# The opening of a gated cross-attention and expert layer: tiles 0 and 1 multiplied before they are scaled, and a new split of the contexts' low parts

## The reference

```python
x = x + tanh(g_xattn) * xattn(layernorm(x), itok, ctx, ctx, ctx)
x = x + tanh(g_ffn) * ffn(layernorm(x), ...)
# xattn: each token has one of 4 experts e, by its id
g = silu(h @ ctx[e].T)
u = h @ ctx[e].T
y = (g * u) @ ctx[e].T
```

## Time and profile before

| | us |
|---|---|
| median of 3 runs | 477.32 (476.93 to 477.61) |
| the profiled execution, its time | 476.73 |
| its span, first to last instruction | 474.9 |
| busy: TensorE (PE), its weight loads (PEld) | 458.2, 393.2 |
| busy: VectorE (DVE), ScalarE (ACT), GpSimd (POOL) | 316.9, 268.1, 212.5 |
| mean granted clock of TensorE | 0.996 |

### The profile page before, as it was taken

How to read it: one execution, slowest core, us unless ns; L and a number is a source line. 1 busy time by engine, 2 the same in 40 slices (tenths; PEclk the granted TensorE clock), 3 DMA queues, 4 the chain that set the end, 5 groups by cost and what they waited for, 6 DMA issues and landing times.

```text
span 474.9 us, 7916 instructions
## 1 busy us (share of the span) xinstructions
PE 458.2 (96%) x2493; PEld 393.2 (83%) x2493; DVE 316.9 (67%) x789; ACT 268.1 (56%) x417; POOL 212.5 (45%) x175
## 2 busy tenths in 40 slices
PE   2999999999999999999999999999999999999993
PEld 1478888888888888888889999999999999999982
DVE  6679888878876554479469776566666676666520
ACT  4766556666564643633345676566655577656431
POOL 0513444664543475426168354443435455443242
PEclk9999999999999999999999999999999999999998
DMA  8643874776664542254289999889879998888555
GB/s 297 196 171 126 267 262 165 235 257 205 241 209 151 179 155 95 55 68 63 35 230 172 284 307 270 252 272 287 268 197 262 247 274 273 266 245 223 110 63 72
DMA packets 29166, 95.04 MB, mean 200 GB/s; under 512 B 4816, under 2 KB 5328, under 8 KB 28624
## 3 DMA queue, kind: packets, MB, share of 16 engines
q0 software_dynamic: 17040, 43.66, 37.4%
q1 hardware_dynamic: 11808, 50.98, 32.1%
q10 hardware_dynamic: 288, 0.01, 0.0%
HBM read 67.50 MB, written 28.70 MB: 203 GB/s over the span
## 4 chain that ended last, share of the span: by engine, by line
PE 95%; ACT 1%; DVE 1%; DMA 1%; POOLq 0%; POOL 0%; issue 0%
PE psG L1314 51%; PE psY L1314 32%; PE psT L1319 8%; PE psG L1572 1%; PE psG L1343 1%; DMA tok_i<-in_ids 1%; PE psY L1331 1%; ACT arena L563 0%; POOLq L81 0%; ACT arena L554 0%; PE psY L1450 0%; PE psG L1344 0%; POOL out L513 0%; PE psY L1476 0%; PE psG L1319 0%
## 5 line engine op out<-in xcount | busy, mean ns | idle before, releaser
L1314 PE MATMUL psY<-arena 128*128 (+1 forms) x372 | 90.8, 394 | 0.0
L1314 PEld LDWEIGHTS psY<-arena 128*128 128x128 f32 x372 | 68.7, 188 | 14.1 <-issue 0.2
L504 POOL DMA_INDIRECT ht<-out,idx x32 | 33.7, 1052 | 59.0 <-PE psT L1319 43.2
L1314 PE MATMUL psY<-slot,arena 128*128 128x512 f32 x240 | 58.8, 394 | 0.0
L1089 DVE TENSOR_TENSOR slot<-raw,slot 128x1536 fp32r<-128x1536 f32 x25 | 43.9, 1757 | 19.5 <-ACT slot L635 19.5
L1314 PE MATMUL psG<-arena 128*128 x228 | 56.8, 398 | 0.0
L1089 DVE TENSOR_TENSOR arena<-raw,arena 128x1536 fp32r<-128x1536 f32 x24 | 42.0, 1758 | 16.4 <-ACT arena L635 16.3
L1314 PEld LDWEIGHTS psY<-slot,arena 128*128 128x128 f32 x240 | 44.2, 188 | 9.2 <-ACT xh_sb L679 0.3
L1314 PE MATMUL psG<-arena,slot 128*128 128x512 f32 x216 | 51.3, 392 | 0.0
L1314 PEld LDWEIGHTS psG<-arena 128*128 128x128 f32 x228 | 41.5, 188 | 8.3 <-issue 0.4
L750 ACT ACTIVATE s_sb<-psG 128x224 f32<-128x224 f32 (+1 forms) x48 | 17.6, 366 | 54.6 <-PE psG L1314 54.6
(11 more groups left out here) (231 smaller groups left out, 814.6 us busy)
## 6 DMA issues: line engine op xcount, KB each, us to landing
raw<-in_w SPq DMA_DIRECT2D x51, 768.0 KB, 5.9
padded<-xh_sb SPq DMA_DIRECT2D x19, 256.0 KB, 2.3
raw<-in_ctx_t SPq DMA_DIRECT2D x2, 1024.0 KB, 8.7
ht<-in_ctx_t SPq DMA_DIRECT2D x1, 1024.0 KB, 11.7
xh_sb<-in_ctx_t SPq DMA_DIRECT2D x1, 1024.0 KB, 7.1
out<-log_sb SPq DMA_DIRECT2D x4, 256.0 KB, 7.6
ht<-out,idx POOLq DMA_INDIRECT x32, 5.2
xb<-in_x,idx POOLq DMA_INDIRECT x19, 3.8
```

The costliest lines, as they stand in the source:

```text
L504: pool.indirect_dma_start(ht[:, n, :], None, halves_of_out, slots(e * NA + a, 0)).then_inc(g_here[n], 16)
L1314: ins = pe.matmul(ps, left[a], right[b], start=n == 0 and m == 0, stop=n == total - 1 and m == 2)
```

## The change

- Tiles 0 and 1 are no longer normalised ahead of their product. VectorE subtracts the mean only (`centre`) into h; ScalarE's and VectorE's passes behind the product take the root as a scale (`silu1`, `gate1`, with `r01`). Their normalising on ScalarE goes. The roots of tiles 0 and 1 are taken as a pair, those of tile 2 alone.
- Tile 1 has its own buffers for its transposed parts (`hT1` in bl0) and bank for its product (psG[1]); TensorE's transposition of tile 1 stands in the middle of tile 0's product, tile 1's product directly behind.
- Low parts: contexts 0 and 1 half by VectorE (`low_ctx(0, 1, 2)`, `low_ctx(1, 0, 2)`, first in its queue) and half by TensorE, two pieces each; context 2 in two halves by VectorE; context 3 whole by VectorE in step 2, ahead of tile 4's statistics, with gate 2 and the low part of tile 3 ahead of it. Four of TensorE's eight pieces go.
- ScalarE takes context 2's high part in two halves, and context 3's directly behind tile 0's SiLU; then come tile 0's gT, tile 2's normalising, and so on.
- Context 3 is loaded into raw, over context 0, and waits for that context's low part besides.
- The steps begin at t = 1; what is before them is written out.

```diff
-            for t in range(FIRST, LAST):
+            for t in range(1, LAST):
...
+        hT1 = [bl0[:, n * KD * P:(n + 1) * KD * P] for n in range(2)]
+        def hT_of(t):
+            return hT1 if t == 1 else hT
+        def p_bank(t):
+            return psG[1 if t == 1 else 0][:, :]
...
         def ctx_raw(e):
-            if e < 2:
-                return raw_flat[:, e * KD * D:(e + 1) * KD * D]
-            return (ht if e == 2 else xh_sb)[:, :, :].rearrange("p a d -> p (a d)")
+            if e == 2:
+                return ht[:, :, :].rearrange("p a d -> p (a d)")
+            return raw_flat[:, e % 3 * KD * D:(e % 3 + 1) * KD * D]
...
-            for e in range(E1 - 1):
+            for e in range(E1):
+                if e == E1 - 1:
+                    sp.wait_ge(xa_here[2], 16)
+                    sp.wait_ge(ctx_lo_done, 1)
                 sp.dma_start(ctx_raw(e), ctx_t[e, :, :]).then_inc(ctx_here[e], 16)
-            sp.wait_ge(xa_here[2], 16)
-            sp.dma_start(ctx_raw(E1 - 1), ctx_t[E1 - 1, :, :]).then_inc(ctx_here[E1 - 1], 16)
...
-            def take_rest(e, i):
-                act.wait_ge(rest_ps, e // 2 * KD + i + 1)
-                if e and i == KD - 1:
-                    act.wait_ge(ctx_lo_done, 2)
-                o = (e * KD + i) * D
+            def take_rest(i):
+                act.wait_ge(rest_ps, i + 1)
+                if i % 2:
+                    act.wait_ge(ctx_half, i // 2 + 1)
+                o = (i // 2 * KD + i) * D
                 act.activation(ctx_lo[:, o:o + D], psG[i][:, :],
-                               ACT.Copy).then_inc(rest_taken if i < KD - 1 else ctx_lo_done, 1)
-            high_ctx(0)
-            high_ctx(1)
-            take_rest(0, 0)
-            take_rest(0, 1)
-            high_ctx(2)
-            take_rest(0, 2)
-            take_rest(0, 3)
+                               ACT.Copy).then_inc(ctx_lo_done if i % 2 else rest_taken, 1)
+            def half_ctx(e, n):
+                act.wait_ge(ctx_here[e], 16)
+                c = slice(n * KD * D // 2, (n + 1) * KD * D // 2)
+                ins = act.activation(ctx_hi[:, e * KD * D:(e + 1) * KD * D][:, c], ctx_raw(e)[:, c], ACT.Copy)
+                if n:
+                    ins.then_inc(ctx_hi_done, 1)
...
+            def hT_high(t):
+                act.wait_ge(hT_ps, t + 1)
+                act.activation(hT_of(t)[0], psT[0][:, :], ACT.Copy).then_inc(hT_hi, 1)
+            def silu1(t):
+                act.wait_ge(p_ps, t + 1)
+                if t:
+                    act.wait_ge(gu_ready, t)
+                if t < 2:
+                    act.wait_ge(r01_ready, t + 1)
+                    act.activation(s_sb[:, 0:D], p_bank(t), ACT.Silu, scale=r01[:, t:t + 1]).then_inc(s_ready, 1)
+                else:
+                    act.activation(s_sb[:, 0:D], p_bank(t), ACT.Silu).then_inc(s_ready, 1)
+            def norm_h(t):
+                act.wait_ge(norm_ready, columns_normed(t - 2) - (1 if t >= 4 and t - 4 < NT else 0))
+                act.wait_ge(hT_ps, t - 1)
+                norm(h[:, t % 2, :], xa_of(t - 2, t % 2, t - 2), 0, h_ready)
...
+            high_ctx(0)
+            high_ctx(1)
+            for i in range(KD - 1):
+                take_rest(i)
+            hT_high(0)
+            take_rest(KD - 1)
+            half_ctx(2, 0)
+            hT_high(1)
+            half_ctx(2, 1)
+            silu1(0)
+            high_ctx(3)
             def step(t, par, known):
                 if have(known, -1):
                     act.wait_ge(gT_ps, t)
                     act.activation(gT[0], psT[1][:, :], ACT.Copy).then_inc(gT_hi, 1)
+                if known == 1:
+                    norm_h(2)
+                    hT_high(2)
...
-                if known == 1:
-                    high_ctx(3)
...
                 if have(known, 0):
-                    act.wait_ge(p_ps, t + 1)
-                    if had(known, 0):
-                        act.wait_ge(gu_ready, t)
-                    act.activation(s_sb[:, 0:D], psG[0][:, :], ACT.Silu).then_inc(s_ready, 1)
-                if have(known, 1):
-                    act.wait_ge(hT_ps, t + 2)
-                    act.activation(hT[0], psT[0][:, :], ACT.Copy).then_inc(hT_hi, 1)
-                if known == -1:
-                    take_rest(2, 1)
-                    take_rest(2, 2)
-                if known == 0:
-                    take_rest(2, 3)
+                    silu1(t)
+                if have(known, 1) and known != 1:
+                    hT_high(t + 1)
                 if have(known, 2):
-                    act.wait_ge(norm_ready, columns_normed(t) - (1 if have(known, -2) else 0))
-                    if had(known, 1):
-                        act.wait_ge(hT_ps, t + 1)
-                    norm(h[:, par, :], xa_of(t, par, known), 1 if known == 0 else 0, h_ready)
-                if known == FIRST:
-                    take_rest(2, 0)
+                    norm_h(t + 2)
...
+                def root01(col, V, Y, T, R, B):
+                    return dve.scalar_tensor_tensor(r01[:, col:col + 1], T, 5 * RS_W ** 2, Y, ALU.add, ALU.mult)
...
-                if pair:
-                    low_h(t, known)
                 each(square)
                 each(third)
-                if had(known, 2):
+                if pair:
+                    each(root01, last=r01_ready)
+                    return
+                if known and had(known, 2):
                     dve.wait_ge(h_ready, t + 2)
                 if had(known, -2):
                     dve.wait_ge(xh_ready, t - 2)
                 each(root)
-                each(offset, last=True)
-            def low_h(t, known):
-                dve.wait_ge(hT_hi, t + 2)
-                dve.tensor_tensor(hT[1], psT[0][:, :], as_f32(hT[0]), ALU.subtract).then_inc(hT_lo, 1)
+                each(offset, last=norm_ready)
...
+            def low_h(t):
+                dve.wait_ge(hT_hi, t + 1)
+                hi, lo = hT_of(t)
+                dve.tensor_tensor(lo, psT[0][:, :], as_f32(hi), ALU.subtract).then_inc(hT_lo, 1)
+            def low_g(t):
+                dve.wait_ge(gT_hi, t + 1)
+                dve.tensor_tensor(gT[1], psT[1][:, :], as_f32(gT[0]), ALU.subtract).then_inc(gT_lo, 1)
+            def gate1(t):
+                dve.wait_ge(s_ready, t + 1)
+                if t:
+                    dve.wait_ge(gT_ps, t)
+                if t < 2:
+                    dve.scalar_tensor_tensor(gu[:, 0:D], p_bank(t), r01[:, t:t + 1], s_sb[:, 0:D],
+                                             ALU.mult, ALU.mult).then_inc(gu_ready, 1)
+                else:
+                    dve.tensor_tensor(gu[:, 0:D], s_sb[:, 0:D], p_bank(t), ALU.mult).then_inc(gu_ready, 1)
...
+            def centre(t):
+                dve.tensor_scalar(h[:, t, :], xa[:, t, :], mv[:, t, 0:1], None, ALU.subtract).then_inc(h_ready, 1)
+            low_ctx(0, 1, 2).then_inc(ctx_half, 1)
+            low_ctx(1, 0, 2).then_inc(ctx_half, 1)
+            stats_of(0)
+            mean_of(0, 0)
+            centre(0)
+            stats_of(1)
+            low_h(0)
+            mean_of(1, 1)
+            centre(1)
+            roots(-1, 1, -1, False, False, True)
+            low_h(1)
+            stats_of(2)
+            gate1(0)
+            mean_of(2, 0)
+            roots(0, 0, 0, True, False, False)
+            link(low_ctx(2, 0, 2))
+            low_g(0)
+            dve.wait_ge(ctx_lo_done, 2)
+            low_ctx(2, 1, 2).then_inc(ctx_lo_done, 1)
+            low_h(2)
...
             def step(t, par, known):
-                one, two = have(known, 2) and known != 0, have(known, -2)
+                one, two = have(known, 2), have(known, -2)
+                if known == 2:
+                    low_g(1)
...
+                if known == 2:
+                    gate1(2)
+                    low_h(3)
+                    dve.wait_ge(ctx_lo_done, 3)
+                    low_ctx(3, 0, 1).then_inc(ctx_lo_done, 1)
+                if known == 1:
+                    gate1(t)
                 if one:
...
+                    stats_of(t + 2)
+                if have(known, -1) and known > 2:
+                    low_g(t - 1)
...
                 if one:
-                    dve.wait_ge(stats_done, NORMS(k, known))
...
+                    mean_of(t + 2, 0)
...
                 if one or two:
-                    roots(t, par, known, one, two, pair)
-                if have(known, 0) and known != 0:
...
-                if have(known, 1) and known not in (FIRST + 1, 0):
-                    low_h(t, known)
-                if pair:
-                    dve.wait_ge(ctx_lo_done, 1)
-                    low_ctx(1, 0, 1).then_inc(ctx_lo_done, 1)
-                if known in (1, 2):
-                    if known == 2:
-                        dve.wait_ge(ctx_lo_done, 3)
-                        low_ctx(3, 1, 2).then_inc(ctx_lo_done, 1)
-                        dve.wait_ge(ctx_lo_done, E1)
-                    else:
```

(92 more changed lines are left out.)

31 lines of the change are left out of this document (removed).

## The result

The changed kernel took 484.81 us (median of 6 runs, 483.19 to 487.00), the kernel before on the same chip 477.53 (6 runs, 476.93 to 478.00): a ratio of 1.0157, 95% interval 1.0131 to 1.0184. Forecast were 484.7, range 480.5 to 486.7. The profiled execution is the longest of the six: 487.00, its span 485.1, its mean granted clock 0.981, where the other five had 0.985 to 0.994. So its parts add up to 10.2 us over the span before, and the median's difference is 7.3.

A forecast was written before the change was run, and what follows sets the result against it. TensorE, busy 96% of the span, was taken to bound the kernel. The profiled 476.73 us plus 4.9 for T h4's delay and 2.5 for the clock made 484.1; the median's 0.59 more gave 484.7, range 480.5 to 486.7.

The forecast's parts named there:

- The bound: Whole run: TensorE, 96% busy, bounds the kernel; whatever moves it in the opening moves the end by as much.
- The gain at the start: Opening up to T g0: TensorE's pieces go and T h0 starts earlier, putting the change over 5 us ahead.
- First wait: T g0 to T h2: context 3 ahead of tile 0's gate on ScalarE makes TensorE wait 3.7 us.
- Second wait: T g2 to T h4: VectorE work ahead of tile 4's statistics makes TensorE wait 5.6 us; T h4 4.9 later.
- The clock: Behind the second wait: TensorE's clock falls to half and the slow work costs 2.5 us; chance 0.57.
- The first fall: Behind the first wait: the clock may fall there too, costing about 0.1 us.
- No fall of the clock: Rival, behind the second wait: only the wait is paid, 482.3 us; chance 0.34.
- Swallowed: Rival, opening: ScalarE and VectorE keep ahead of TensorE, the 4.36 us of pieces simply go, 473.0 us; chance 0.05.
- no change: Rival, opening: all of ScalarE's waits gone, T h4 at 41.7, time 477.4 us; chance 0.04.

The follow-up runs named there:

- VectorE's order alone undone: Changed kernel with gate 2, the low part of tile 3 and context 3's low part moved behind tile 4's roots on VectorE; 480.28 us.
- the second wait filled: Changed kernel plus 16 matmuls into an unread bank between T g2 and T h4; 482.27 us, repeated as a companion 483.17 us.
- both filled: Changed kernel plus 8 unread matmuls between T g0 and T h2 and 16 between T g2 and T h4; 483.29 us.
- ScalarE's order undone: Changed kernel with context 3's high part moved behind tile 1's SiLU on ScalarE; 483.86 us.
- the reordered kernel: Changed kernel's arithmetic, ScalarE's and VectorE's queues both reordered, context 3's low part in two halves; 477.47 us, ratio to before 0.9997.
- low part 3 moved once more: Kernel with both queues reordered, context 3's low-part halves moved ahead of x1(1) and tile 5's statistics; 476.61 us, ratio to before 1.0000.

## Why the prediction was right

- *The bound.* Right. The change of T h4 and the clock's loss behind it appear unchanged 415 us later (8.85 and 8.81), so what moves TensorE in the opening moves the end. Not seen was that something lies behind TensorE's end: the last adds on GpSimd, which wait for the adds ahead of them to land, worth 1.4 us in the profiled execution.
- *The gain at the start.* Right: T h0 forecast at 17.5 and measured at 17.68, G0 19.6 and 19.97, G1 22.9 and 23.66, T g0's end 26.1 and 27.1. VectorE's two half subtractions (2.35 us) filled its idle time. The centring takes 0.49, not 0.4, without effect.
- *First wait.* Right in its mechanism: context 3 ahead of gT(0), T h2 forecast at 29.8 and measured at 30.49. The term that was off is the landing, taken at 26.5 and measured at 27.3: SP issued the transfer at 19.20, not at 18.72, and it took 8.1 us, not the 7.8 reckoned. That ScalarE's order makes the wait, the run with context 3 behind tile 1's SiLU shows.
- *Second wait.* Right: tile 4's statistics forecast at 42.5, came at 43.86; T h4 forecast at 46.54, came at 47.48; 4.9 against 5.9 us. The 0.9 between the two times of T h4 is the sum of three errors: T h2 came 0.7 late with the landing; from T h2 to the statistics it took 0.7 longer than reckoned, 0.45 of it the slow T h2; and the chain from the statistics to T h4 took 3.6 us, not 4.0. The wait itself was forecast as 5.6 and is 4.0, because T g2 ended later too, behind a slow Y0. VectorE's order alone undone gave back 4.5 us.
- *The clock.* The size was right, the argument behind it was not. Forecast 2.5, measured 2.9 along the chain of the profiled execution (2.7 against the execution with the wait filled) and 1.8 to 2.4 by the ratios. But the step said that the clock falls 4.3 us after the last work and that the wait of 5.6 is longer than that. Both figures were off: the last work before ended at 467.71, so that the clock fell 3.0 us after it, and the wait was 4.0. By 4.3 a wait of 4.0 should not have brought a fall; it did, 3.0 us after T g2. By 3.0 the clock was to be expected to fall in the first wait too, forecast at 3.7, where the step has only a "may".
- *The first fall.* Mis-sized: "about 0.1" because Y0 and G2 lie beside the round of ScalarE and VectorE. They do, but T h2 lies in that round, and its 0.45 us more count in full: 0.45 to 0.6.
- *The rivals.* "No fall of the clock" would have been 482.3. With the second wait filled the kernel measured 482.27 and 483.17, with both filled 483.29, so its number was near; in the profiled execution its condition was not met. In the fastest of the six runs, 483.19 with a mean clock of 0.994, it may have been. "Swallowed" and "no change" needed tile 4's statistics at about 37.5; they came 6.4 us later. They do come early when both orders are changed (33.61 in the first such version), and even then the 4.36 us of pieces taken from TensorE are not 4.36 us of time.

The median fits to 0.1 partly by luck: in the profiled execution the steps were 1.0 (T h4), 0.4 (clock) and 1.4 (the end) too small, and that execution is 2.2 above the median. The mean clocks of the six runs, 0.981 to 0.994, suggest that the falls were not of one size, while the sum has one figure for them.

## What to carry to other kernels

Work taken off the engine that bounds the run counts only if the other engines bring the next inputs as much earlier; here 4.36 us were taken off TensorE, and a 2.28 us subtraction queued ahead of a tile's statistics, with a fixed chain of 3.6 us between these and TensorE's next work, turned that into a loss. So after such a change look first at what stands in the other queues ahead of the start of the next tile's chain: moving five lines in VectorE's queue was worth 4.5 of 7.3 us. Price a wait of TensorE with the slow work behind it: here 4.0 us of wait had some 2 to 3 us of loss at half clock behind them.

## What was not expected of the hardware

- The clock falls at uneven times after TensorE's last matmul: 3.0 us after it at the end of the kernel before; 2.3 and 3.0 in the changed kernel; 2.1 in the kernel with the second wait filled (27.4 to 29.5), in a wait of 2.46; 2.6 in the kernel with ScalarE's order undone (40.5 to 43.1); and 4.6 in the kernel with VectorE's order undone (27.4 to 32.0), with T h2 already begun. It did not fall in waits of 1.74 and 1.39.
- It stayed low for 6.8 us both times in the changed kernel, though TensorE was at work for most of that; in the kernel with the second wait filled only from 29.5 to 32.9, in that with VectorE's order undone from 32.0 to 35.4. A wait can thus have about twice as long a slow stretch behind it in one execution as in another, which fits with the scatter of the changed kernel, 3.8 us over six runs against 1.1 before, and with the mean clocks of these runs; that was not tried apart.
- Transfers of the same size take different times in different executions. Context 3 took 7.1 us before, 8.1 in the changed kernel, and from 6.7 to 9.1 in the kernels with its queues changed or its waits filled; the rows gathered near 161 us took 3.4 before and 4.5 in the reordered kernel; the slower of the last-but-one pair of adds took 4.9 before, 6.2 in the changed kernel and 5.8 in the kernel with low part 3 moved once more. A lead of 1 to 2 us in front of them does not reach the end whole. Why a transfer takes longer in some executions stays open.
